# A decoder on one core: another order of the latent attention's steps on TensorE, VectorE and ScalarE, and a one-element silu in the delta attention

## What is computed

```python
q_hk = (hidden_q @ Wq.T).reshape(Bv, Sv, H, K)
q_big = jnp.einsum('bshk,hkq->bshq', q_hk, w_kc_q)
...
q_big = _apply_rope(q_big, sin_q[None, :, None, :], cos_q[None, :, None, :])
...
q_r = jnp.einsum('bshq,hqr->bhsr', q_big, W_qr)
k_r = jnp.einsum('bld,hdr->bhlr', kv_r, W_kr)
scores = jnp.einsum('bhsr,bhlr->bhsl', q_r, k_r)
attn = jax.nn.softmax(scores, axis=-1)
ctx_c = jnp.einsum('bhsl,bld->bhsd', attn, kv_r)
ctx_lat = jnp.einsum('bhsd,hkd->bhsk', ctx_c, w_kc_kv)
ctx = ctx_lat.transpose(0, 2, 1, 3).reshape(Bv, Sv, H * K)
return ctx @ Wo.T
```

## Time and profile before

| | |
|---|---|
| median of three runs | 1599.18 us |
| lowest and highest | 1598.6 and 1601.16 us |
| the profiled execution | 1597.62 us |
| its span | 1595.7 us |
| mean granted TensorE clock | 0.904 of 2.4 GHz |
| TensorE busy | 1301.9 us, 82% |
| VectorE busy | 847.9 us, 53% |
| ScalarE busy | 495.8 us, 31% |
| GpSimd busy | 515.3 us, 32% |

### The profile page before, as it was taken

How to read it: one execution, slowest core, us unless ns; L and a number is a source line. 1 busy time by engine, 2 the same in 40 slices (tenths; PEclk the granted TensorE clock), 3 DMA queues, 4 the chain that set the end, 5 groups by cost and what they waited for, 6 DMA issues and landing times. The chain is left out here.

```text
span 1595.7 us, 24725 instructions
## 1 busy us (share of the span) xinstructions
PE 1301.9 (82%) x9098; PEld 838.1 (53%) x9098; DVE 847.9 (53%) x1857; ACT 495.8 (31%) x1157; POOL 515.3 (32%) x596
## 2 busy tenths in 40 slices
PE   5999999832691787999999875788888887999998
PEld 2758577521351454666676763344444444444477
DVE  4463645347139566676764345556554565373334
ACT  0505224120022576666664311233333333100000
POOL 1533526141642467546753112211111111050000
PEclk9999999856795798999999777999999998999999
DMA  3000100490485202212211102000002000554100
GB/s 115 21 16 17 33 13 0 172 273 8 126 224 172 70 14 41 32 29 35 35 24 23 23 0 53 23 24 24 24 24 62 22 1 1 165 178 128 51 4 23
DMA packets 168742, 92.66 MB, mean 58 GB/s; under 512 B 91392, under 2 KB 161768, under 8 KB 168512
## 3 DMA queue, kind: packets, MB, share of 16 engines
q1 hardware_dynamic: 160912, 76.65, 18.2%
q0 software_dynamic: 4496, 13.33, 2.8%
q10 hardware_dynamic: 3232, 1.31, 0.3%
HBM read 76.82 MB, written 15.79 MB: 58 GB/s over the span
## 5 line engine op out<-in xcount | busy, mean ns | idle before, releaser
L2615 PE MATMUL la_banks<-la_xe,la_f_w 128*128 128x512 f32 x348 | 151.4, 593 | 3.4 <-DVE la_xe L3017 3.4
L1933 DVE SCALAR_TENSOR_TENSOR dh_front<-dh_pj,df_conv,dh_front 128x510 f32<-128x510 f32 x144 | 107.4, 746 | 73.2 <-ACT dh_front L1673 69.5
L3181 POOL TENSOR_TENSOR la_area<-la_area 128x512 f32<-128x512 f32 x48 | 60.4, 1273 | 259.1 <-DVE la_area L2874 196.3
L2615 PEld LDWEIGHTS la_banks<-la_xe,la_f_w 128*128 128x128 f32 x348 | 65.4, 190 | 83.6 <-issue 83.5
L2748 ACT ACTIVATE la_area<-la_banks,la_nmax 128x256 f32<-128x256 f32 x128 | 58.9, 472 | 144.4 <-DVE la_nmax L2883 144.4
L2410 PE MATMUL la_banks<-xT,la_area 128*128 128x512 f32 x192 | 91.7, 604 | 1.0 <-ACT la_area L2732 1.0
L330 POOL TENSOR_TENSOR wa_qkT<-wa_t_cos,wa_t_sin 128x512 f32<-128x512 f32 x40 | 50.8, 1270 | 123.8 <-DVE wa_t_sin L306 123.8
L3017 DVE TENSOR_TENSOR la_xe<-xT,la_area 128x1024 f32<-128x1024 f32 x29 | 52.5, 1827 | 55.5 <-PE la_banks L2615 48.1
L342 ACT ACTIVATE wa_capped<-wa_lg 128x384 f32<-128x384 f32 x64 | 31.2, 488 | 161.3 <-PE wa_lg L258 159.9
L2452 PE MATMUL la_banks<-const,la_area 128*128 128x128 f32 x256 | 41.5, 289 | 45.6 <-DVE la_area L2894 30.1
L334 POOL TENSOR_TENSOR wa_masked<-wa_probs,const 128x384 f32<-128x384 f32 x64 | 63.8, 1000 | 40.7 <-ACT wa_probs L345 40.7
(11 more groups left out here) (551 smaller groups left out, 3007.4 us busy)
## 6 DMA issues: line engine op xcount, KB each, us to landing
placed<-mw_rows SPq DMA_DIRECT2D x8, 768.0 KB, 7.8
mw_gu<-in_L_ffn_w_gate SPq DMA_DIRECT2D x16, 384.0 KB
mw_gu<-in_L_ffn_w_up SPq DMA_DIRECT2D x16, 384.0 KB
mw_d<-in_L_ffn_w_down SPq DMA_DIRECT2D x16, 384.0 KB, 7.7
mw_rows<-placed SPq DMA_DIRECT2D x8, 768.0 KB, 5.3
la_area<-w_table POOLq DMA_DIRECT2D x6, 1024.0 KB, 11.6
la_f_w<-in_L_ffn_q_proj SPq DMA_DIRECT2D x32, 128.0 KB, 2.2
la_f_w<-in_L_ffn_k_proj SPq DMA_DIRECT2D x32, 128.0 KB, 2.4
```

The source lines that it names most:

```text
L1933: dve.scalar_tensor_tensor(dst, src[:, :, 0:SEQ - j], conv[:, a, m, D_CONV - 1 - j:D_CONV - j], dst, ALU.mult, ALU.add).then_inc(tapped, 1)
L2615: mm = pe.matmul(acc[c][m], f_w[n % SLOTS][:, m, k, :], xe[(n - U) % RING][:, k, :], start=first and k == 0, stop=last and k == KC - 1)
L3181: pool.tensor_tensor(qrot[:, c, n, :], prod[:, c, 2 * n, :], prod[:, c, 2 * n + 1, :], ALU.add).then_inc(rotated, 1)
```

## The change

In the latent attention the same calls stand in another order in all three lists; none is added or dropped. Scores, maximum and exponentials of batch 0 of a pair move from the iteration after the pair's queries into that iteration (`scores(i, 0)`, `maximum(i, 0)`, `exp(i, 0)` near its end), and the turns, attends, outputs and norms shift by some places. A memset of `lpad` moves from behind VectorE's loop to the stage's start. In the delta attention a silu of one column of a constant, `early`, which nobody reads, is put between `exp(a, 1)` and `tap0(a, 3)`.

```diff
@@ -1139,6 +1139,7 @@
         a_exp = sb("a_exp", [P, D_H])
...
+        early = sb("early", [P, 1])
         vT = [sb(f"vT{q}", [P, 2, SEQ]) for q in range(4)]
         wo_s, wg_s, nw = sb("wo", [P, 3, DIM]), sb("wg", [P, KC, D_N]), sb("nw", [P, 1])
         osq, ms, orstd = sb("osq", [P, TILES, D_V]), sb("ms", [P, D_H, TILES]), sb("orstd", [P, D_H, TILES])
@@ -1824,6 +1825,7 @@
                     if a is not None:
                         exp(a, 0)
                         exp(a, 1)
+                        act.activation(early[:], env.c("ident")[:, 0:1], ACT.Silu)
                         tap0(a, 3)
                     for n in news[1:2]:
                         taps_v(n)
@@ -2492,8 +2494,6 @@
                 output_weights(0)
                 for i in range(PAIRS):
                     j = i - 1
-                    if j >= 0:
-                        scores(j, 0)
                     queries(i, 0, 0)
                     if j >= 1:
                         outputs(j - 1, 2)
@@ -2502,47 +2502,46 @@
                         outputs(j - 1, 3)
                     if j >= 0:
                         scores(j, 1)
+                        turn(j, 0, 0)
                     queries(i, 0, 2)
                     if j >= 0:
-                        turn(j, 0, 0)
+                        turn(j, 0, 1)
                     queries(i, 1, 0)
                     if j >= 0:
-                        turn(j, 0, 1)
+                        attend(j, 0)
+                        turn(j, 1, 0)
                         scores(j, 2)
                     queries(i, 1, 1)
                     if j >= 0:
-                        attend(j, 0)
-                        turn(j, 1, 0)
+                        turn(j, 1, 1)
                     latent_queries(i, 0)
                     if j >= 0:
-                        turn(j, 1, 1)
+                        attend(j, 1)
+                        turn(j, 2, 0)
                     queries(i, 1, 2)
                     if j >= 0:
-                        attend(j, 1)
                         scores(j, 3)
-                        turn(j, 2, 0)
+                        turn(j, 2, 1)
+                        attend(j, 2)
                     latent_queries(i, 1)
-                    if j >= 0:
-                        turn(j, 2, 1)
-                        outputs(j, 0)
-                        attend(j, 2)
-                        outputs(j, 1)
-                    if i + 1 < PAIRS:
+                    if i < LAST:
                         absorb(i + 1)
                     if j >= 0:
+                        outputs(j, 0)
                         turn(j, 3, 0)
-                    if i + 1 < PAIRS:
+                        outputs(j, 1)
+                    scores(i, 0)
+                    if j >= 0:
+                        turn(j, 3, 1)
+                    if i < LAST:
                         output_weights(i + 1)
                     if j >= 0:
-                        turn(j, 3, 1)
                         attend(j, 3)
-
+                scores(LAST, 1)
                 outputs(LAST - 1, 2)
-                scores(LAST, 0)
-                outputs(LAST - 1, 3)
-                scores(LAST, 1)
                 turn(LAST, 0, 0)
                 turn(LAST, 0, 1)
+                outputs(LAST - 1, 3)
                 scores(LAST, 2)
                 attend(LAST, 0)
                 turn(LAST, 1, 0)
@@ -2759,27 +2758,25 @@
                 for i in range(PAIRS):
                     j = i - 1
                     if j >= 0:
-                        exp(j, 0)
+                        copy_eT(j, 0, 0)
                         exp(j, 1)
-                        copy_eT(j, 0, 0)
                         copy_eT(j, 0, 1)
+                        copy_eT(j, 1, 0)
                         exp(j, 2)
-                        copy_eT(j, 1, 0)
+                        copy_eT(j, 1, 1)
                     copy_qc(i, 0)
                     if j >= 0:
-                        copy_eT(j, 1, 1)
+                        copy_eT(j, 2, 0)
                         exp(j, 3)
-                        copy_eT(j, 2, 0)
+                        copy_eT(j, 2, 1)
                     copy_qc(i, 1)
-                    if j >= 0:
-                        copy_eT(j, 2, 1)
-                    if i + 1 < PAIRS:
+                    if i < LAST:
                         copy_absorbed(i + 1)
                     if j >= 0:
                         copy_eT(j, 3, 0)
+                    exp(i, 0)
+                    if j >= 0:
                         copy_eT(j, 3, 1)
-
-                exp(LAST, 0)
                 exp(LAST, 1)
                 copy_eT(LAST, 0, 0)
                 copy_eT(LAST, 0, 1)
@@ -2911,6 +2908,7 @@
                     ins.then_inc(step, 1)
                     dve.wait_ge(step, count[0])
 
+                chain(dve.memset(lpad[:], NEG))
                 dve.wait_ge(sim_summed, 1)
...
                 copy_mo(0)
@@ -2921,16 +2919,15 @@
                 chain(dve.reciprocal(thr[:, 1, :], thr[:, 1, :]))
                 for i in range(PAIRS):
                     j = i - 1
-                    if j >= 0:
-                        maximum(j, 0)
                     rope(i, 0, 0)
                     if j >= 1:
                         add(j - 1, 2)
+                    if j >= 0:
+                        norm(j, 0)
                     rope(i, 0, 1)
                     if j >= 1:
                         add(j - 1, 3)
                     if j >= 0:
-                        norm(j, 0)
                         maximum(j, 1)
                     rope(i, 0, 2)
                     rope(i, 1, 0)
@@ -2938,15 +2935,17 @@
                         norm(j, 1)
                         maximum(j, 2)
                     rope(i, 1, 1)
+                    if j >= 0:
+                        norm(j, 2)
                     rope(i, 1, 2)
                     if j >= 0:
-                        norm(j, 2)
                         maximum(j, 3)
                         copy_cx(j, 0)
                         add(j, 0)
                         norm(j, 3)
                         add(j, 1)
-                    if i + 1 < PAIRS:
+                    maximum(i, 0)
+                    if i < LAST:
                         copy_mo(i + 1)
                     if j >= 0:
                         copy_cx(j, 1)
@@ -3082,12 +3081,10 @@
                     dve.wait_ge(o_rstd_ready, t + 1)
...
 
-                chain(dve.memset(lpad[:], NEG))
-                maximum(LAST, 0)
+                maximum(LAST, 1)
                 add(LAST - 1, 2)
-                maximum(LAST, 1)
+                norm(LAST, 0)
                 add(LAST - 1, 3)
-                norm(LAST, 0)
                 maximum(LAST, 2)
                 norm(LAST, 1)
                 maximum(LAST, 3)
```

## The result

The changed kernel takes 1633.1 us (median, 1630.53 to 1633.45) against 1599.18: **2.1% slower**, ratio 1.0206 with a 95% interval of 1.0189 to 1.0224. The forecast was 1634. Its profiled execution took 1632.8 us, span 1630.7. The total is right to 1 us, and that is luck: it is the sum of two terms that were both wrong, in opposite directions. For the latter: the latent attention's first matmul starts at 957.33 instead of 976.80, 19.5 sooner, of which 1.9 was there before the delta attention began (its first table load for silu is at 520.70 instead of 522.58). That leaves 17.6, but not all of it is the silu's.

A forecast was written before the change was run, and what follows sets the result against it. In the latent attention TensorE is busy 84.9 of 100 us, so only its idle time and clock count. Latent attention +43 and early silu -8 give +35 on 1597.6, or 1632.6; with 1.6 for the median 1634 us, range 1612 to 1656.

The forecast's parts named there:

- The work of 35.9: Latent attention: TensorE's work in one 44.09 us iteration without gaps and clock loss, 35.9 us, left alone by the change.
- the five gaps: Latent attention, new TensorE waits: attend(j,2) 4.4, attend(j,3) 2.8, turn(j,3,0) 2.1, turn(j,1,0) 1.8, turn(j,2,0) 0.25; together 11.35 against 6.48.
- +43: Latent attention's whole loss in us: 6.6 more in each of five whole iterations, plus the first and last pairs.
- the 0.25: Wait before turn(j,2,0) in the latent attention, shrinking from 2.39 to 0.25 us, norm(j,2) still beside GpSimd's additions.
- Two falls in an iteration: Latent attention: clock falls to 1.2 GHz behind the 4.4 and 2.8 gaps, costing 3.4 us an iteration instead of 1.7.
- a 2.08: Gap near the latent attention's end that left the next group at full clock; grounds for no fall behind 2.1.
- "more clock loss" rival: Latent attention: three clock falls an iteration instead of two, kernel at 1646 us; chance 0.2.
- The silu term: Delta attention: table load moved ahead of the last tap0 shrinks TensorE's waits for silu; -8 us taken.
- the bound of -14: Delta attention, low bound of the early silu: shorter waits also spare clock falls, 3 of 1.7 us.
- The Trainium skill's drain: Delta attention: some 1.4 us added to each table load; by it tap0 1.8 late and the silu's part +2.
- lpad: Its memset, moved to the latent stage's idle start, costs nothing, since VectorE waits there anyway.
- The rival "faster": Latent attention: late engines recover, three other gaps (6.7 us) vanish, kernel 1578 us; decided at turn(j,3,0); chance 0.08.

The follow-up runs named there:

- fillers: Changed kernel plus matmuls nobody reads in its three longest gaps, ahead of attend(j,2), turn(j,3,0) and attend(j,3): 1596.52 us, ratio 0.9993 to the kernel before.
- the last kernel: Changed kernel with attend(j,2), scores/exp(i,0), turn(j,1,0) and the turns and attend behind it later, norm(j,3) ahead of add(j,0): 1504.94 us, ratio 0.947.
- the latent part alone: Changed kernel without the early silu: 1648.07 us, ratio 1.0323 to the kernel before.
- the two single kernels: Kernel before with only the early silu: 1582.85 us, ratio 0.9897; changed kernel without that silu: 1648.07 us, ratio 1.0323.
- the kernel with the later silu: Kernel before with the early silu behind the last tap0 instead of ahead of it: 1583.87 us beside 1586.17, ratio 0.9992.

## Why the prediction was right in its total and wrong in two terms

- **The work of 35.9 and the five gaps** (4.4, 2.8, 2.1, 1.8, 0.25) held: 4.24, 2.60, 2.04, 1.63 and 0.65. The iteration with fillers (46.9 for 47.25) and the last kernel (36.15 with 0.71 of gaps, 35.4 of work) show both halves of the sum. Of the forecast's +43, 31 was idle time; measured 30.
- **The miss among the gaps** is the 0.25. The four scalings took 3.05 us beside GpSimd's additions, not the 2.58 of the earlier trace rows; the gap is 0.65. The prediction read the earlier trace rows as four scalings of 0.65 each, "not one of them held for a whole addition". One by one they take 0.78, 1.35, 0.34 and 0.34 there, beside additions of 1.27 and 1.32 us: two are held until an addition ends, and two run free. In the changed kernel it is 1.25, 1.35, 0.34 and 0.34; the first starts 0.16 behind the first addition and not 0.64, which is the 0.47 more. The Trainium skill (SBUF — State Buffer, section "SBUF: two separate sides") has the shared port locked for the whole instruction; the trace agrees, a scaling of 0.34 taking 1.35 beside an addition of 1.31. The prediction worked out from that rule an end 0.8 later, a gap of 1.05. That was its own working and too much: with two scalings held, the last one ends 0.67 behind the second addition, as it did in the earlier trace rows (0.68).
- **The clock failed.** "Two falls in an iteration ... and none behind 1.8 and 2.1: 3.4 instead of 1.7" put the clock's part of the +43 at 12. Measured it is 24. Both halves of that step were wrong: a fall does follow the 2.04 in the changed kernel, which the single row of a 2.08 without one had talked me out of, and a fall costs up to 3.0 and not 1.7, since it reaches the whole of latent_queries (4.59 for 2.84) or of four queries (3.78 for 1.98) besides the attend. The "more clock loss" rival (three falls, 1646) comes nearer to what the latent attention did: +54 and -8 would have given 1597.6 + 54 - 8 + 1.6 = 1645. But only half of the whole iterations have three falls; the rest is that a fall is dearer than the 1.7 of the forecast.
- **The silu term failed on the other side**: some -14 in what repeats (-16.5 by the runs) for -8. The items of that sum make -8.4 and not the -9 written there, which changed nothing. In the six settled iterations between the turns at 655.45 and 819.28 (650.57 and 802.45 after) it is 12 us and not 6.6: the left-over wait is 0 and not 0.25, and the half-clock groups behind every second wait went, some 1.5 us three times. That was in the forecast as the bound of -14 "if the shorter waits also spare the clock falls", and I gave it no part of the value, although the intervals of 26.6 and 28.1 us between the turns of before show it. Another 2 to 2.6 come behind the last turn, where I had nothing: a wait of TensorE for an addition of VectorE (3.1 us in the kernel before, 2.8 in that with the latent part alone) is 0.4 to 1.1 in the nine kernels with the early silu ahead of tap0. Why, no run shows. Of the first heads nothing certain can be said: up to the first settled turn these two traces differ by 3.0 (forecast 1.8), and two traces of the same delta attention by 5.8. The waits of the second and third head did fall, from 4.57 to 4.23 and 4.14, where I had counted a loss of 0.2 each. The Trainium skill's drain (ScalarE: Activation LUTs, section "What ACT_TABLE_LOAD costs") was not seen: the early silu starts 1.29 behind its load, and tap0 0.11 behind that.
- **Both errors have in the main one root**: I priced the idle time by walking the queues and the clock by the one gap that the earlier trace rows show. In the latent attention that left out 12 us of cost, in the delta attention some 4 of gain.
- **The total** had a second piece of luck: the spans of the two traces differ by 35.0 us, 5 less than +54 and -14 make. The 5 lie ahead of the settled heads (1.9 and 3.0), where traces of the same code differ as much.
- **lpad** at nothing, and that the two parts don't disturb each other: no run tells the memset apart, and the sum of the two single kernels (+35.1, to about 10 us) matches the whole (+34).
- **The rival "faster"** fell for the reason given: the outputs of TensorE start the chain of the 2.04, and no engine ran ahead.

## What to carry to other kernels

In a hand-ordered set of queues, walk each engine's list once and write the gap of every waiting instruction; here that gave five gaps to 0.4 us each, and shifting one call by one place (attend(j, 2)) was worth 1.8%. Then price the clock apart, as a range: here a gap of 4.24 was followed by half clock every time, gaps of 1.87 to 2.60 in some iterations and not in others, and even shorter ones now and then; which of two neighbouring gaps takes the fall changed from one iteration to the next. And where an engine stands idle for about as long as a table load takes, a dummy of one column puts the load there; the same dummy one call later won half as much in the settled heads and nothing that the whole time could show.

## What the runs showed of the chip that I had not expected

- Unread matmuls in three gaps made the kernel 2.1% faster (ratio 0.9993 against 1.0206), though they free no other engine: they are worth 4.2 to 7.6 us in each iteration, by the clock alone.
- Half clock followed gaps of 1.87 and 2.04 us in some iterations and not in others of the same kernel: 4.54 us of latent_queries behind a 1.87 in one kernel and 2.84 behind the same 1.87 in the one before it. A gap of 1.34 us in the delta attention was followed by it every second time, one of 0.88 once in the kernel with the later silu, and in the latent attention of the kernel before one of 0.68, close behind one of 0.95, once in seven iterations (the attend at 1227.65 takes 1.75 for 1.08, the scores behind it 2.08 for 1.13). What decides is not settled by these runs. They show that of two neighbouring gaps one may take the fall and spare the other, and that there was none in the iterations shown whose gaps were 0.28 and 0.43 (the last kernel), or 0.80, 0.71, 0.61, 1.63 and 0.65 (the one with fillers).
- Four scalings of VectorE took 2.58 us beside GpSimd's additions in the kernel before and 3.05 in the changed one, 1.14 alone. The whole surplus is in the first two: each lasts until the addition beside it ends (1.35 us beside 1.31), and the row of four hides that.
